# The second residual's addition on GpSimd instead of VectorE, with the layer norm statistics behind it as a step of their own

## The chip, the cores and the metric

One core of one Trainium2 chip runs the whole program. The metric is the device time of one execution in microseconds (us), and less is better. The engines are TensorE (PE in the profile, its weight loads PEld), VectorE (DVE), ScalarE (ACT), GpSimd (POOL) and SyncE (SP), which issues nearly all DMAs. Each works through its own queue of instructions in order and waits on semaphores for the others.

## The reference

Two layers work on x of shape 2 x 2048 x 512 in float32. The first has attention to a context of 128 rows and a feed-forward part with ternary weights. The second has a linear mixing part and a quantised feed-forward part. The piece that matters here is the second residual of the first layer and what reads it:

```
h  = bitlinear(ln2, w_fc) + gate * low_rank(ln2)
x2 = r1 + tanh(g_ffn[0]) * bitlinear(relu(h) ** 2, w_proj)   # second residual
y  = (x2 - mean(x2)) / sqrt(var(x2) + 1e-5)                  # the second layer's norm
x3 = x2 + tanh(g_xattn[1]) * (y @ W1.T + part2 + b)          # third residual
```

Here r1 is the result of the first residual (x plus the gated attention), and the layer norms have no weights.

## The kernel before, in words

The 4096 rows of x are cut into 16 groups of 256 rows, g = 0 to 15, and each group into two tiles t = 0, 1 of 128 rows. A tile of activations is 128 partitions x 512 float32. The weights are prepared in about the first 130 us, partly beside the first groups. From then on some four groups are under way at once: while one group is in its attention, the one before is in the first feed-forward part and older ones are in the second layer.

No scheduler runs on the chip. The table `ORDER` holds for each engine, each kind of step, each group and each tile the place of that step in the engine's queue. `moments` and `due` turn the table into the queues at build time, and each engine's `run` calls the steps in the order of those places. At one place a step may issue several instructions.

The steps around the change, for tile t of group g:

- `down` on PE multiplies the squared hidden values with w_proj into PSUM bank `FFN0 + t` and signals `down_ps`.
- `x2_out` on VectorE (lines 1454 to 1463) multiplies that bank with the row scales `scbc` into `r2` (line 1459) and signals `down_mul`; `low_rows` and `up` of the next group on PE wait for this signal, since they write the same banks. Then it adds `r1` to `r2` in place (line 1461), signals `x2_done`, and goes on in the same step to `ln_stats` (lines 1369 to 1374: statistics, a one-column memset, aggregate, and variance plus epsilon into `ve`).
- `rs3` on GpSimd (line 749) raises `ve` to the power -0.5 into `rs`.
- `ln3_apply` on VectorE (line 1378) forms the normalised `x3n`, ScalarE makes the float16 high part, `x3_lo` on GpSimd (line 753) the low part, SP turns both with a DMA transpose, and `mix` on PE multiplies them.
- `add_cb` on GpSimd (line 788) adds the context row `cb` to `r2` after `ln3_apply`.

GpSimd also runs `x1_lo` and `x2_lo` (line 753, low parts of the first and second normalised input), `hid` (line 776), `norm` (line 781), `rot` (line 771), `add_b2` (line 794) and the other `rs` steps. For the last group `r2_of` gives `xb` and the transposes are made by PE.

Of the kernel before, what the change touches and what calls it, by code (L numbers as in the profile page):

```python
# [48 lines left out]
def build(nc, x_d, ctxT_d, wqT_d, wkvT_d, woT_d, wfc_d, wproj_d, uT_d, wxT_d, wcT_d, bx_d, w1T_d, b1_d, w2T_d, b2_d,  # L49
          rope_d, small_d, out_d):  # L50
    ctx = ExitStack()
    with ctx:
# [278 lines left out]
        def last_in(place):  # L331
# [49 lines left out]
                rot_lo=((24, 27), (69, 70), (114, 115), (164, 165), (214, 215), (261, 265), (310, 312), (359, 361),  # L381
                        (410, 411), (456, 457), (505, 507), (554, 555), (602, 603), (653, 654), (704, 705),
                        (750, 751)),
                rot=((21, 25), (64, 66), (111, 112), (162, 163), (212, 213), (259, 262), (306, 309), (356, 358),
                     (407, 408), (452, 453), (502, 504), (552, 553), (600, 601), (650, 651), (702, 703),
                     (744, 745)),
                sum=((36, 39, 44, 45), (77, 80, 82, 84), (120, 132, 134, 135), (171, 173, 174, 183),
# [3 lines left out]
                max=((31, 32, 33, 38), (73, 74, 75, 76), (117, 121, 122, 124), (166, 167, 168, 169),  # L391
# [3 lines left out]
                p_lo=((40, 41, 47, 50), (87, 92, 93, 96), (123, 137, 138, 140), (175, 176, 180, 187),  # L395
# [3 lines left out]
                pv=((51, 57), (99, 105), (142, 144), (191, 192), (237, 242), (291, 292), (330, 339), (380, 389),  # L399
                    (434, 435), (486, 488), (536, 537), (584, 586), (627, 633), (682, 683), (730, 731), (779, 780)),  # L400
                x1=((59, 61), (107, 109), (149, 151), (197, 198), (246, 249), (295, 296), (342, 344), (393, 396),
                    (441, 442), (491, 493), (540, 542), (589, 591), (638, 640), (687, 688), (739, 740), (783, 785)),
                ln2=((60, 63), (110, 113), (150, 153), (199, 200), (248, 250), (298, 299), (346, 347), (395, 397),
                     (444, 445), (495, 496), (544, 547), (593, 594), (642, 643), (690, 691), (741, 742),
                     (787, 788)),
                low=((83,), (118,), (160,), (206,), (258,), (307,), (354,), (403,), (455,), (506,), (556,), (604,),
                     (652,), (697,), (749,), (796,)),
                q4=((119, 128), (170, 181), (211, 226), (260, 276), (314, 329), (362, 379), (409, 432), (466, 469),
                    (512, 523), (564, 570), (612, 619), (657, 665), (700, 711), (756, 770), (795, 798), (819, 822)),
                x3=((116, 125), (161, 177), (209, 220), (257, 271), (311, 324), (353, 375), (406, 425), (459, 468),  # L410
                    (508, 519), (558, 567), (608, 615), (649, 663), (699, 709), (753, 762), (793, 797), (818, 820)),
                h=((129, 130, 131, 133, 136, 146, 147, 148), (178, 184, 185, 186, 188, 189, 195, 201),
# [7 lines left out]
                q5_sc=((139, 157), (190, 207), (241, 251), (289, 303), (338, 357), (390, 401), (433, 449),  # L420
                       (485, 498), (535, 546), (583, 597), (632, 645), (679, 693), (728, 746), (775, 786),
                       (805, 809), (828, 833)),
                q5=((141, 159), (193, 210), (244, 255), (293, 305), (340, 360), (392, 404), (436, 451), (487, 500),
                    (538, 550), (585, 598), (634, 647), (681, 694), (738, 748), (781, 789), (806, 811), (832, 834)),
                x4=((154, 172), (205, 216), (253, 264), (304, 318), (350, 369), (402, 418), (454, 462), (499, 514),
                    (549, 563), (596, 609), (646, 656), (692, 706), (747, 757), (791, 794), (816, 821), (835, 836)),
                ln3=((104, 108), (145, 158), (196, 203), (240, 263), (301, 308), (343, 355), (387, 405), (440, 458),
                     (492, 503), (541, 551), (590, 605), (637, 655), (686, 701), (729, 752), (784, 792),
                     (812, 815)),
                x2=((102, 106), (143, 156), (194, 202), (238, 256), (294, 302), (341, 352), (385, 399), (437, 450),  # L430
                    (490, 501), (539, 548), (588, 599), (635, 648), (684, 695), (727, 743), (782, 790), (810, 813)),
                ln1_st=((0, 1), (14, 16), (62, 67), (126, 152), (179, 204), (221, 252), (272, 297), (327, 345),
                        (376, 398), (427, 443), (471, 494), (522, 543), (573, 592), (617, 641), (685, 696),
                        (732, 733)),
                ln1=((2, 4), (17, 18), (65, 68), (127, 155), (182, 208), (225, 254), (280, 300), (332, 348),
                     (382, 400), (431, 446), (475, 497), (526, 545), (579, 595), (625, 644), (689, 698),
                     (734, 735))),
# [41 lines left out]
                x1_lo=((2, 3), (9, 10), (30, 31), (73, 83), (107, 121), (139, 152), (173, 183), (209, 219),  # L479
                       (243, 254), (278, 286), (312, 319), (344, 353), (378, 388), (412, 422), (453, 459),  # L480
                       (486, 487)),
                x2_lo=((28, 29), (51, 55), (78, 82), (114, 115), (147, 149), (181, 182), (217, 218), (249, 251),
                       (285, 287), (321, 322), (355, 356), (387, 389), (421, 424), (454, 455), (490, 491),
                       (521, 522)),
                x3_lo=((49, 50), (76, 87), (111, 119), (144, 158), (185, 191), (214, 225), (246, 258), (281, 293),
                       (315, 327), (349, 361), (384, 395), (417, 431), (450, 465), (483, 498), (520, 525), (0, 0)),
                rot=((11, 12), (25, 26), (52, 54), (90, 92), (127, 129), (156, 157), (188, 190), (224, 227),
                     (259, 262), (290, 291), (324, 326), (359, 360), (392, 393), (428, 429), (467, 468),
                     (493, 494)),
                norm=((14, 15, 16, 17), (32, 33, 34, 35), (58, 70, 71, 72), (97, 98, 99, 105), (135, 136, 137, 140),  # L490
# [83 lines left out]
        def due(eng, name, p):  # L574

            return placed.get((eng, name, p), ())
# [1428 lines left out]
```

## Time and profile before

| what | value |
| --- | --- |
| median of 3 runs | 1177.62 us (1175.28 to 1179.0) |
| the profiled execution's own time | 1178.83 us |
| span of its instructions | 1176.7 us |
| PE busy | 1094.3 us, 93% |
| VectorE busy | 953.5 us, 81% |
| ScalarE busy | 799.4 us, 68% |
| GpSimd busy | 591.5 us, 50% |

The span runs from the first to the last instruction of the profiled execution. Its own time is 2.1 us longer, for what lies around the instructions, and is 1.2 us above the median of the runs. Busy time counts an engine's instructions without its waits, so a share well under 100% says nothing by itself about which wait sets the end.

### The profile page before, as it was taken

To read this page: it belongs to the slowest core of one execution; us is meant where nothing else is said; L and a number is where in the kernel's file an instruction comes from. 1 tells how busy PE (TensorE), PEld (TensorE's weight loads), DVE (VectorE), ACT (ScalarE), POOL (GpSimd) and SP (SyncE) were. 2 spreads that over 40 slices of the span, in tenths; PEclk is the share of its full clock that TensorE was granted. 3 is DMA by queue.
4 is the path that set the end of the run, shared out by engine and by line. 5 is a ranking of instruction groups with operands and counts; after the bars stand their busy time and mean duration, and the time that the engine had idled before them with its cause. 6 is when DMAs were issued, how large, how long until landed. Compare 5 with 4: busy or idle time off the path is not lost.

```text
span 1176.7 us, 22172 instructions
## 1 busy us (share of the span) xinstructions
PE 1094.3 (93%) x8270; PEld 677.4 (58%) x8558; DVE 953.5 (81%) x1989; ACT 799.4 (68%) x1575; POOL 591.5 (50%) x567
## 2 busy tenths in 40 slices
PE   5776699999999999999899999999999999999997
PEld 5544456474655656475655656475656656564654
DVE  4796868778789888788878798898879886998667
ACT  3988947676683958576584857676674957586545
POOL 4243545464653746454544656555545555564431
PEclk9888799999999999999999999999999999999999
DMA  9959651434525343533625252443436242432210
GB/s 339 367 153 309 204 122 47 99 81 77 126 59 117 69 116 73 104 81 68 126 53 136 57 123 68 89 110 77 108 55 145 45 119 61 103 69 55 68 45 27
DMA packets 273802, 128.11 MB, mean 109 GB/s; under 512 B 247568, under 2 KB 248080, under 8 KB 272016
## 3 DMA queue, kind: packets, MB, share of 16 engines
q1 hardware_dynamic: 273136, 125.73, 41.8%
q8 instruction: 67, 1.10, 0.4%
q10 hardware_dynamic: 560, 0.96, 0.3%
q14 instruction: 39, 0.32, 0.1%
HBM read 57.19 MB, written 8.39 MB: 56 GB/s over the span
## 4 chain that ended last, share of the span: by engine, by line
PE 55%; ACT 17%; DVE 16%; POOL 5%; issue 4%; DMA 2%; SPq 0%; ACTq 0%; DVEq 0%
PE ps L1861 14%; PE ps L1835 10%; PE ps L1904 6%; PE ps L1920 5%; PE ps L1788 5%; ACT e L966 4%; PE ps L1735 4%; PE ps L1883 4%; ACT rl L1002 3%; ACT hid L1007 2%; ACT sq L1013 2%; PE ps L1760 1%; DVE st L1369 1%; PE ps L1841 1%; PE ps L1775 1%
## 5 line engine op out<-in xcount | busy, mean ns | idle before, releaser
L1835 PE MATMUL ps<-xT,fcT 128*128 128x256 f16 x2048 | 262.5, 276 | 10.8 <-ACT rl L1002 7.1
L749 POOL TENSOR_TENSOR rs<-ve,nhalf 128x1 f32<-128x1 f32 x160 | 101.7, 638 | 306.1 <-DVE ve L1374 222.8
L1861 PE MATMUL ps<-pjT,hid 128*128 128x512 fp8e4 x1024 | 232.3, 379 | 2.6 <-POOL hid L776 1.6
L1835 PEld LDWEIGHTS ps<-xT,fcT 128*128 128x128 fp8e4 x2048 | 200.1, 99 | 52.6 <-ACT rl L1002 10.0
L776 POOL TENSOR_TENSOR hid<-sq,hid 128x512 f16<-128x512 f32 x128 | 163.1, 1279 | 80.3 <-ACT sq L1013 79.4
L1861 PEld LDWEIGHTS ps<-pjT,hid 128*128 128x128 f16 x1024 | 98.0, 98 | 98.3
L1002 ACT ACTIVATE rl<-ps,rsf 128x256 f32<-128x256 f32 x256 | 106.4, 469 | 25.0 <-PE ps L1841 24.8
L966 ACT ACTIVATE e<-ps,nmb,sig 128x128 f32<-128x128 f32 x256 | 113.1, 462 | 7.2 <-DVE nmb L1412 6.9
L1904 PE MATMUL ps<-w1T,q4T 128*128 128x512 fp8e4 x480 | 114.2, 379 | 0.7 <-issue 0.6
L1058 ACT ACTIVATE q<-h 128x2048 f16<-128x2048 f32 x30 | 57.3, 1910 | 79.3 <-DVE h L1531 79.3
L781 POOL TENSOR_TENSOR e<-e,einv 128x512 f32<-128x512 f32 x64 | 70.1, 1100 | 78.5 <-DVE einv L1416 78.5
L1520 DVE SCALAR_TENSOR_TENSOR h<-ps,dqs,b1bc 128x512 f32<-128x512 f32 x120 | 87.4, 744 | 27.0 <-PE ps L1904 24.4
L1920 PE MATMUL ps<-w2T,hT 128*128 128x512 fp8e4 x480 | 108.5, 379 | 0.7 <-DMA hT<-q 0.7
L1735 PE MATMUL ps<-pt,wq 128*128 128x256 f16 x768 | 88.6, 275 | 4.4 <-DVE r L1434 3.0
L1788 PE MATMUL ps<-wo,qT 128*128 128x512 f16 x384 | 87.3, 384 | 4.4 <-DVE qT L1382 4.4
L1735 PEld LDWEIGHTS ps<-pt,wq 128*128 128x128 f16 x768 | 75.3, 99 | 18.4 <-issue 7.8
L1883 PE MATMUL ps<-wx,xT 128*128 128x512 f16 x360 | 82.5, 379 | 2.3 <-DVE r L1556 1.2
L1007 ACT ACTIVATE hid<-rl 128x512 f16<-128x512 f32 x128 | 80.6, 630 | 5.0
L1100 DVE TENSOR_REDUCE amax<-h 128x1 f32<-128x2048 f32 x30 | 68.4, 2280 | 13.4 <-ACT h L1027 13.3
L1013 ACT ACTIVATE sq<-rl 128x512 f32<-128x512 f32 x128 | 78.5, 613 | 0.0
L1920 PEld LDWEIGHTS ps<-w2T,hT 128*128 128x128 f16 x480 | 46.2, 98 | 50.7
L1382 DVE TENSOR_TENSOR p<-e,p 128x512 f16<-128x512 f32 x64 | 62.6, 993 | 14.0 <-ACT p L974 13.7
(243 smaller groups left out, 2025.7 us busy)
## 6 DMA issues: line engine op xcount, KB each, us to landing
xb<-in_x SPq DMA_DIRECT2D x16, 512.0 KB, 3.6
xa<-in_x SPq DMA_DIRECT2D x15, 512.0 KB, 4.0
out<-r SPq DMA_DIRECT2D x30, 256.0 KB, 2.3
rope<-in_rope SPq DMA_DIRECT2D x16, 384.0 KB, 3.2
h<-in_w1T SPq DMA_DIRECT2D x6, 1024.0 KB, 5.8
h<-in_w2T SPq DMA_DIRECT2D x6, 1024.0 KB, 6.4
h<-in_wkvT SPq DMA_DIRECT2D x2, 1024.0 KB, 12.6
hid<-in_w_fc SPq DMA_DIRECT2D x2, 1024.0 KB, 9.9
```

The costliest lines, as they stand in the source:

```text
L776: pool.tensor_tensor(flat[:, 1, :], sq[:, m % 2, :], flat[:, 0, :], ALU.subtract).then_inc(hid_lo, 1)
L966: last = act.activation(e[:, n, a * S:(a + 1) * S], s_bank(g, n)[:, a * S:(a + 1) * S], ACT.Exp, bias=nmb[:, n, a:a + 1], scale=sig[:, :], ...
L1002: act.activation(rl[:, m % 2, a * G:(a + 1) * G], ps[:, FFN0 + m % 2, a * G:(a + 1) * G], ACT.Relu, scale=rsf[:, 2 * m + a:2 * m + a + 1]) ...
L1007: act.activation(hid[:, 0, 2 * m:2 * m + 2, :].rearrange("p c n -> p (c n)"), rl[:, m % 2, :], ACT.Square)\
L1013: act.activation(sq[:, m % 2, :], rl[:, m % 2, :], ACT.Square).then_inc(sq_done, 1)
L1735: mm = pe.matmul(q_bank(hg)[:, a * G:(a + 1) * G], wq[:, ws, k, c:c + P], xT1[:, xs, k, :], start=(n == 0 and k == 0), stop=(n == 2 and k ...
L1788: mm = pe.matmul(wo_bank(t), ao[:, xs, k, t * P:(t + 1) * P], wo[:, ws, k, :], start=(n == 0 and k == 0), stop=(n == 2 and k == KC - 1))
L1835: pe.matmul(ps[:, FFN0 + m % 2, a * G:(a + 1) * G], fcT[:, k, f * P:(f + 1) * P], xT2[:, xs, k, :], start=(xs == 0 and k == 0), stop=False)
L1861: mm = pe.matmul(ps[:, FFN0 + t, :], hid[:, xs, c, t * P:(t + 1) * P], pjT[:, c, :], start=(c == 0 and xs == 0), stop=(c == FC - 1 and xs ...
L1883: mm = pe.matmul(mix_bank(g, t), xT3_of(g)[:, xs, k, t * P:(t + 1) * P], wx[:, ws, k, :], start=(n == 0 and k == 0), stop=(n == 2 and k == ...
L1904: mm = pe.matmul(mix_bank(g, 2 + u), q4T_of(g)[:, k, t * P:(t + 1) * P], w1T[:, k, n * 512:(n + 1) * 512], start=(k == 0), stop=(k == KC - 1))
L1920: mm = pe.matmul(mix_bank(g, 10 + t), hT_of(g)[:, t, c, :], w2T[:, c, :], start=(c == 0), stop=(c == FC - 1))
```

## The change

On VectorE the addition of `r1` is taken out of `x2_out`, and the statistics become a step `x2_st` of their own. On GpSimd a new step `add_r1` makes the addition. The semaphores are the same: `add_r1` waits for `down_mul` and signals `x2_done`, and `x2_st` waits for `x2_done`. There are 32 of each, two for every group. Apart from the two new rows of the table, every engine runs its steps in the sequence that it had before; only the numbers of the places are shifted. PE, ScalarE and SP keep their places unchanged.

```diff
             DVE=dict(
+                x2_st=((103, 108), (146, 160), (199, 208), (245, 264), (303, 312), (352, 364), (398, 413),
...
             POOL=dict(
+                add_r1=((44, 47), (77, 86), (113, 121), (148, 160), (185, 193), (221, 231), (256, 266), (293, 304),
...
+            def add_r1(g, t):
+                need(pool, down_mul, TILES, g, t)
+                pool.tensor_tensor(r2_of(g)[:, t, :], r2_of(g)[:, t, :], r1[:, g % 2, t, :], ALU.add).then_inc(x2_done, 1)
+
...
                     for t, g in due("POOL", "x3_lo", p):
                         x3_lo(g, t)
+                    for t, g in due("POOL", "add_r1", p):
+                        add_r1(g, t)
...
                 need(dve, down_ps, TILES, g, t)
                 dve.tensor_tensor(r2_of(g)[:, t, :], ps[:, FFN0 + t, :], scbc[:, :], ALU.mult).then_inc(down_mul, 1)
-                need(dve, down_mul, TILES, g, t)
-                dve.tensor_tensor(r2_of(g)[:, t, :], r2_of(g)[:, t, :], r1[:, g % 2, t, :], ALU.add).then_inc(x2_done, 1)
+
+            def x2_stats(g, t):
                 need(dve, x2_done, TILES, g, t)
                 ln_stats(ln3, g, 2, t, r2_of(g)[:, t, :], 1.0, EPS)
...
                         x2_out(g, t)
+                    for t, g in due("DVE", "x2_st", p):
+                        x2_stats(g, t)
```

Where the new steps stand is shown at two places. The first is VectorE's queue around `x2_out` of group 8, tile 0 (about 685 us in the profile). Before, the multiplication, the addition (r<-r) and the statistics follow each other:

```order
L1531 TENSOR_SCALAR h<-h,qsc 128x2048
L1382 TENSOR_TENSOR qT<-ps,qT 128x2x256
L1520 SCALAR_TENSOR_TENSOR h<-ps,dqs,b1bc 128x512
L1459 TENSOR_TENSOR r<-ps,scbc 128x512
L1461 TENSOR_TENSOR r<-r 128x512
L1369 BN_STATS st<-r 128x6
L1371 MEMSET pad 128x1
L1372 BN_AGGR mv<-st 128x2
L1374 TENSOR_SCALAR ve<-mv 128x1
L1434 SCALAR_TENSOR_TENSOR r<-ps,kapo,xb 128x512
```

In the changed kernel the same stretch reads so, with lines shifted by 12:

```order
L1543 TENSOR_SCALAR h<-h,qsc 128x2048
L1394 TENSOR_TENSOR qT<-ps,qT 128x2x256
L1532 SCALAR_TENSOR_TENSOR h<-ps,dqs,b1bc 128x512
L1471 TENSOR_TENSOR r<-ps,scbc 128x512
L1381 BN_STATS st<-r 128x6
L1383 MEMSET pad 128x1
L1384 BN_AGGR mv<-st 128x2
L1386 TENSOR_SCALAR ve<-mv 128x1
L1446 SCALAR_TENSOR_TENSOR r<-ps,kapo,xb 128x512
```

The addition has gone, and nothing was put between the multiplication and the statistics. This holds at all 32 places: `x2_st` is the very next step behind its `x2_out`.

The second place is GpSimd's queue around the same step of group 13, tile 1 (about 1022 us), with `x1_lo` (x16a) and `x2_lo` (x16f) of group 14. Before:

```order
L753 TENSOR_TENSOR x16a<-xa,x16a 128x512 x2
L749 TENSOR_TENSOR rs<-ve,nhalf 128x1 x2
L753 TENSOR_TENSOR x16f<-rl,x16f 128x512 x2
L749 TENSOR_TENSOR rs<-ve,nhalf 128x1
L771 TENSOR_TENSOR e<-e 128x512 x2
```

In the changed kernel, where lines are shifted by 6 and L792 is the new addition:

```order
L759 TENSOR_TENSOR x16a<-xa,x16a 128x512 x2
L755 TENSOR_TENSOR rs<-ve,nhalf 128x1 x2
L759 TENSOR_TENSOR x16f<-rl,x16f 128x512
L792 TENSOR_TENSOR r<-r 128x512
L759 TENSOR_TENSOR x16f<-rl,x16f 128x512
L755 TENSOR_TENSOR rs<-ve,nhalf 128x1
L777 TENSOR_TENSOR e<-e 128x512 x2
```

Here the addition stands between the two `x2_lo` of group 14. At 27 of the 32 places it stands directly ahead of the `rs3` of its own tile. At the other five (tile 1 of groups 1, 4, 9, 13 and 14) another step of GpSimd lies between, in groups 9, 13 and 14 the `x2_lo` of the next group's tile 1.

## Rows read from the trace of the kernel before

**Rows 1.** The page: busy time of each engine, share of the span, instructions.

```profile
PE 1094.3 (93%) x8270; PEld 677.4 (58%) x8558; DVE 953.5 (81%) x1989; ACT 799.4 (68%) x1575; POOL 591.5 (50%) x567
```

**Rows 2.** Windows of the span: start and end, us, busy us of each engine, clock, DMA.

```profile
400.00:500.00 100.00, 98.09 (x702) 57.99 (x732) 83.23 (x166) 68.69 (x129) 54.53 (x52) 1.00 0.44 96
...
1000.00:1100.00 100.00, 97.59 (x685) 55.34 (x712) 88.43 (x185) 63.05 (x109) 51.15 (x50) 1.00 0.38 86
```

**Rows 3.** The chain that ended last, shares by engine and by line, from the page.

```profile
PE 55%; ACT 17%; DVE 16%; POOL 5%; issue 4%; DMA 2%; SPq 0%; ACTq 0%; DVEq 0%
```

**Rows 4.** That chain in order of time (start us, us): VectorE's additions on it.

```profile
298.90 0.70 DVE r L1461
...
433.05 1.26 DVE r L1461
...
1004.90 0.70 DVE r L1461
```

**Rows 5.** Lines, by form: count, busy us and mean ns of one, idle time before.

```profile
L749 POOL TENSOR_TENSOR rs<-ve,nhalf 128x1 f32<-128x1 f32 x160 | 101.7, 638 | 306.1 <-DVE ve L1374 222.8 <-DVE ve L1527 68.8 <-DVE ve L1543 14.3
...
L753 POOL TENSOR_TENSOR x16f<-rl,x16f 128x512 f16<-128x512 f32 x32 | 41.6, 1310 | 12.5 <-ACT x16f L984 12.5
...
L794 POOL TENSOR_TENSOR r<-r,b2bc 128x512 f32<-128x512 f32 x30 | 37.9, 1264 | 0.4 <-DVE x3n L1481 0.4
...
L1461 DVE TENSOR_TENSOR r<-r 128x512 f32<-128x512 f32 x30 | 23.0, 767 | 1.0
```

**Rows 6.** Timeline of VectorE, 684 to 690 us (start us, us; idle in brackets).

```profile
685.08 0.67 DVE L1459 TENSOR_TENSOR r<-ps,scbc 128x512 f32<-128x512 f32 x1
685.79 0.69 DVE L1461 TENSOR_TENSOR r<-r 128x512 f32<-128x512 f32 x1
686.51 0.69 DVE L1369 BATCH_NORM_STATS2 st<-r 128x6 f32<-128x512 f32 x1
...
687.46 0.15 DVE L1374 TENSOR_SCALAR ve<-mv 128x1 f32<-128x1 f32 x1
```

**Rows 7.** Timeline of GpSimd in the same stretch.

```profile
682.77 2.14 POOL L753 TENSOR_TENSOR x16a<-xa,x16a 128x512 f16<-128x512 f32 x1
687.70 0.55 POOL L749 TENSOR_TENSOR rs<-ve,nhalf 128x1 f32<-128x1 f32 x1 [2.79 <-DVE ve L1374]
```

**Rows 8.** Timeline of GpSimd, 1018 to 1032 us.

```profile
1021.10 0.80 POOL L749 TENSOR_TENSOR rs<-ve,nhalf 128x1 f32<-128x1 f32 x1 [1.25 <-DVE ve L1374]
1022.30 2.77 POOL L753 TENSOR_TENSOR x16f<-rl,x16f 128x512 f16<-128x512 f32 x2 [0.40 <-ACT x16f L984]
```

**Rows 9.** Timeline of VectorE in that stretch.

```profile
1021.93 0.55 DVE L1378 TENSOR_SCALAR rl<-r,mv,rs 128x512 f32<-128x512 f32 x1 [0.44 <-POOL rs L749]
...
1023.12 0.93 DVE L1461 TENSOR_TENSOR r<-r 128x512 f32<-128x512 f32 x1
```

**Rows 10.** SP's issues and PE there, and time to landing from the DMA view.

```profile
1023.57 2.80 SPq L650 DMA_TRANSPOSE xT<-x16f  x2
...
1028.81 0.40 PE L1801 MATMUL ps<-xT,vcol 128*32 128x256 f16 x8
...
xT<-x16f SPq DMA_TRANSPOSE x32, 2.8
```

**Rows 11.** VectorE, then GpSimd, 430 to 436 us: beside the long addition of the chain.

```profile
434.34 0.69 DVE L1369 BATCH_NORM_STATS2 st<-r 128x6 f32<-128x512 f32 x1
...
432.60 1.15 POOL L753 TENSOR_TENSOR x16a<-xa,x16a 128x512 f16<-128x512 f32 x1
```

**Rows 12.** Waits of PE, 300 to 1100 us: total us, times, longest.

```profile
PE ps L1760 <- DVE qT L1382: 5.7, 6, 2.0
```

**Rows 13.** Chain near the end, then VectorE's row that PE needs there.

```profile
1135.28 3.45 PE ps L1920 x16
...
1138.79 0.63 PE ps L1647 x4
...
1138.10 0.55 DVE L1378 TENSOR_SCALAR e<-xb,mv,rs 128x512 f32<-128x512 f32 x1
```

More of the change, by code:

```diff
@@ L401, in build @@
[L401 to L407, printed above, removed]
@@ L420, in build @@
[L420 to L424, printed above, removed]
@@ new lines, in build @@
+                rot_lo=((24, 27), (69, 70), (116, 117), (168, 169), (220, 221), (269, 273), (320, 322), (371, 373),
+                        (424, 425), (472, 473), (523, 525), (574, 575), (624, 625), (677, 678), (730, 731),
+                        (778, 779)),
+                rot=((21, 25), (64, 66), (113, 114), (166, 167), (218, 219), (267, 270), (316, 319), (368, 370),
+                     (421, 422), (468, 469), (520, 522), (572, 573), (622, 623), (674, 675), (728, 729),
+                     (772, 773)),
@@ new lines, in build @@
+                sum=((36, 39, 44, 45), (77, 80, 82, 84), (122, 134, 136, 137), (175, 177, 178, 187),
[3 rows of a table added]
+                max=((31, 32, 33, 38), (73, 74, 75, 76), (119, 123, 124, 126), (170, 171, 172, 173),
[3 rows of a table added]
+                p_lo=((40, 41, 47, 50), (87, 92, 93, 96), (125, 139, 140, 142), (179, 180, 184, 191),
[3 rows of a table added]
+                pv=((51, 57), (99, 106), (144, 147), (195, 196), (243, 249), (299, 300), (340, 349), (392, 402),
+                    (448, 449), (502, 504), (554, 555), (604, 606), (649, 655), (706, 707), (757, 758), (807, 808)),
@@ new lines, in build @@
+                x1=((59, 61), (109, 111), (152, 154), (202, 203), (253, 256), (304, 305), (353, 355), (406, 409),
+                    (456, 457), (508, 510), (559, 561), (610, 612), (661, 663), (712, 713), (766, 767), (812, 814)),
+                ln2=((60, 63), (112, 115), (153, 156), (204, 205), (255, 257), (307, 308), (357, 358), (408, 410),
+                     (459, 460), (512, 513), (563, 566), (614, 615), (665, 666), (715, 716), (768, 769),
+                     (816, 817)),
+                low=((83,), (120,), (164,), (212,), (266,), (317,), (366,), (417,), (471,), (524,), (576,), (626,),
+                     (676,), (723,), (777,), (826,)),
@@ new lines, in build @@
+                q5_sc=((141, 161), (194, 213), (248, 258), (297, 313), (348, 369), (403, 415), (447, 464),
+                       (501, 515), (553, 565), (603, 618), (654, 668), (703, 718), (755, 774), (803, 815),
+                       (835, 839), (860, 865)),
+                q5=((143, 163), (197, 216), (251, 262), (301, 315), (350, 372), (405, 418), (450, 467), (503, 517),
+                    (556, 570), (605, 619), (656, 670), (705, 719), (765, 776), (809, 818), (836, 842), (864, 866)),
@@ new lines, in build @@
+                ln1_st=((0, 1), (14, 16), (62, 67), (128, 155), (183, 210), (227, 259), (280, 306), (337, 356),
+                        (388, 411), (441, 458), (487, 511), (540, 562), (593, 613), (639, 664), (710, 722),
+                        (759, 760)),
+                ln1=((2, 4), (17, 18), (65, 68), (129, 158), (186, 214), (231, 261), (288, 309), (342, 359),
+                     (394, 414), (445, 461), (491, 514), (544, 564), (599, 616), (647, 667), (714, 724),
+                     (761, 762))),
@@ new lines, in build @@
+                x2_lo=((28, 29), (53, 57), (81, 85), (119, 120), (154, 156), (190, 191), (228, 229), (262, 264),
+                       (300, 302), (338, 339), (374, 376), (408, 410), (444, 447), (479, 480), (517, 519),
+                       (550, 552)),
+                x3_lo=((51, 52), (79, 91), (116, 125), (151, 166), (195, 201), (225, 237), (259, 272), (296, 309),
+                       (332, 345), (368, 381), (405, 417), (440, 455), (475, 491), (510, 526), (549, 555), (0, 0)),
+                rot=((11, 12), (25, 26), (54, 56), (94, 96), (133, 135), (164, 165), (198, 200), (236, 239),
+                     (273, 276), (306, 307), (342, 344), (379, 380), (414, 415), (452, 453), (493, 494),
+                     (521, 522)),
@@ new lines, in build @@
+                norm=((14, 15, 16, 17), (32, 33, 34, 35), (60, 72, 73, 74), (101, 102, 103, 109),
[3 rows of a table added]
+                rs2=((22, 23), (49, 55), (80, 82), (117, 118), (153, 155), (187, 188), (223, 226), (261, 263),
+                     (297, 298), (333, 334), (367, 371), (403, 406), (441, 442), (476, 477), (515, 516),
+                     (545, 547)),
+                rs3=((45, 48), (78, 88), (114, 122), (149, 161), (186, 196), (222, 232), (257, 267), (294, 305),
+                     (330, 341), (366, 377), (402, 413), (438, 449), (472, 483), (507, 520), (544, 553),
+                     (571, 574)),
@@ new lines, in build @@
+                add_b2=((59, 65), (97, 106), (129, 138), (163, 173), (205, 216), (234, 250), (275, 286), (311, 318),
+                        (347, 354), (383, 390), (420, 426), (451, 462), (487, 498), (529, 534), (557, 559),
+                        (577, 579)),
+                rs5=((76, 89), (112, 126), (152, 158), (184, 197), (220, 238), (260, 269), (291, 303), (326, 337),
+                     (364, 373), (399, 411), (436, 446), (469, 481), (508, 523), (542, 548), (565, 569),
+                     (580, 581)),
```

94 lines of the change are left out of this document (30 added, 64 removed), and 52 rows, old and new, of tables (h, hid, max, norm).

## Prediction, made before the changed kernel had run

> **What bounds the kernel now.** I read the page first: PE is busy 93% of the span, VectorE 81%, GpSimd 50% [rows 1]. Such shares are means over a start, a steady part and an end, so I split the span into windows. In the steady part PE is busy 98 of 100 us, VectorE 83 to 88 of 100 [rows 2]. PE is the bound there, and VectorE is the next in line, with little room. Then I read the chain that ended last. PE has only 55% of it, VectorE 16%, ScalarE 17%, GpSimd 5% [rows 3]. PE's long pieces are joined again and again by short stretches over the other engines, which can't be seen in PE's idle time, since PE fills part of them with other work. PE's own waits for VectorE show where these joints hurt: from 300 to 1100 us the largest entry is 5.7 us in six waits for `qT` [rows 12]. So VectorE isn't the bound by its busy time, but a delay of VectorE at the wrong moment is paid.
>
> Next I looked for the step that is changed on the chain. Ten of the 32 additions of line 1461 lie on it, the first at 298.90 and the last at 1004.90 us, one of them a long one of 1.26 us at 433.05 [rows 4]. At these ten places VectorE went through multiplication, addition and statistics without a pause, and the end of the program hung on it.
>
> **What the change removes and adds, on VectorE.** The usual case is in [rows 6]: the multiplication ends at 685.08 + 0.67 = 685.75, the addition takes 0.69, and the statistics start at 686.51, which is 0.76 us behind the multiplication's end. After the change VectorE has nothing between the two and waits for GpSimd. That takes:
> - the hand-over to GpSimd, 0.09 us: `ve` ended at 687.46 + 0.15 = 687.61 and GpSimd's `rs` that waited for it started at 687.70 [rows 6, 7];
> - the addition on GpSimd. This very one isn't in the trace. The nearest row is line 794, the same shape, types and operation with two inputs: 1.26 us [rows 5]. As bounds I take VectorE's own time, 0.69, below, and line 753 of `x16f` with its collisions, 1.31, above [rows 5, 6]. I take 1.26;
> - the hand-over back, 0.03 us: `rs` ended at 1021.10 + 0.80 = 1021.90, and VectorE's instruction behind it started at 1021.93 [rows 8, 9].
>
> The sum is 1.38 us in place of 0.76, so the statistics start **0.62 us later**, and everything that is queued behind them on VectorE with them: in this place the `x1_out` of the next group, for whose sum and norm PE's next low-rank and up products wait. Taking 0.69 us of work from VectorE thus makes VectorE's queue longer, since its place is not filled. The 32 places make 32 x 0.62 = 20 us of delay.
>
> **On GpSimd.** It gets 32 x 1.26 = 40 us more work, 591.5 to about 632 us, still 54% of the span. That alone costs nothing: the `rs` steps wait 306 us in total, 222.8 of it for `ve` [rows 5], and the addition falls into the wait that stood there. In [rows 7] GpSimd ended `x16a` at 682.77 + 2.14 = 684.91, before the multiplication's end, and then sat idle for 2.79 us. At six places it is still at work at that moment by more than a hair, mostly with `x16f`. The worst on the chain is the one at 433.05: `x16a` ends at 432.60 + 1.15 = 433.75, so the statistics would start at 433.75 + 1.26 + 0.03 = 435.04 instead of 434.34 [rows 11], 0.7 later, and 0.8 if the hand-over counts in full. All 32 together come to some 21 us.
>
> In three groups the new addition also stands ahead of the second `x2_lo` of the next group. In group 13 the pair ran from 1022.30 to 1025.07 [rows 8]. With an addition of 1.26 us between them, and the low parts at 1.15 like the undisturbed `x16a` of [rows 11], it ends near 1025.9, 0.8 later. SP turns the result (2.8 us to landing), which was there by about 1027.9, and PE reads it at 1028.81 [rows 10]. The room is 0.9, so nearly used up. I count 0.2 us for it, with 0 to 1 as bounds. No DMA is added or moved on SP; the transposes of x3 start later by the same 0.6 us as the norm.
>
> **A rule on the other side.** The added work on GpSimd also frees VectorE's second read path. The trace shows the collision: the addition takes 0.93 us at 1023.12, while GpSimd is in its `x16f` pair, and 1.26 at 433.05 [rows 4, 9], against 0.69 alone; the group's mean is 767 ns [rows 5]. So the additions lose (0.767 - 0.69) x 30 = 2.3 us this way, and GpSimd's `x16f`, at 1.31 [rows 5] against 1.15 [rows 11], may lose up to 0.16 x 32 = 5.1 us, not all of it by this.
>
> The Trainium skill (SBUF — State Buffer, section Who interferes with whom) says that a VectorE instruction with two SBUF inputs contends with a GpSimd instruction that reads SBUF, and that the one that starts second blocks for the whole of the other. The trace agrees with 0.93 and 1.26 us against 0.69. By this rule alone the change would win up to 2.3 + 5.1 = 7 us; by the sum of waits it loses, and the new GpSimd addition collides with nothing on VectorE, which is waiting for it.
>
> **The sum.** On the chain: nine places x 0.62 = 5.6, and 0.8 for the tenth, 6.4 us. These are paid in full unless the chain is only the last of several equals, and even then a chain made longer stays longer. The last group's second tile adds 0.5: PE's turn of its norm starts at 1138.79, VectorE's row ended at 1138.10 + 0.55 = 1138.65, and PE's work before ended at 1135.28 + 3.45 = 1138.73, so the room is 0.1 us [rows 13]. The shifted `x2_lo` adds 0.2. Of the other 20 places some will become the last to arrive; I take 0.9 us for them, as an estimate, like one and a half of 20 places. Together **8 us**. Against the profiled execution, 1178.83 us, that is 1186.8. The median of the runs is 1.2 us lower, so the forecast is **1185.7 us**.
>
> **Rivals.**
> - *The cover holds.* VectorE's idle time of 12 to 17 us in 100 [rows 2] takes up the 0.62 us before PE needs anything. For it: from one `x2_out` to the next there are some 30 us with about 4 us of idle time. Against it: ten of the places lie on the chain. It would give 0 to 3 us more, 1178 to 1181.
> - *All places are paid.* Each delay reaches PE, because queues written out by hand for one timing have no spare room anywhere. Then 21 us, and 1199 us in the median. For it: PE at 98%, so that nothing lost is given back. Against it: 22 of the 32 additions aren't on the chain. Half-way, at 13 us and more, I count it as this case.
> - *Faster, by fewer collisions.* The mechanism is the read path above: VectorE's additions no longer stop GpSimd's low parts and the reverse. It gives 2 to 7 us less, about 1173 to 1175. It decides if the hand-over and the longer addition cost less than 0.2 us on the chain in each place, thus if GpSimd did the addition in about 0.8 us. Line 794 with 1.26 speaks against it.
>
> **How the numbers follow.** A measurement of this kernel tells about 0.3%, 3.5 us, from no change. The forecast's case (4 to 13 us more) gets 0.62; all places paid 0.14; the cover holds 0.15; faster 0.09. The last two give same 0.15 and faster 0.09, the first two slower 0.76. The range goes from 1179 (the cover nearly holds) to 1195 (17 us more, four fifths of all places); it leaves out the faster case and the upper part of the second rival, some 2 in 10.
>
> **What the new profile would show.** If right: VectorE's statistics on `r` at the new step wait 32 times for GpSimd's new line, 1.3 to 1.4 us each, 42 to 46 us in total; VectorE's busy time falls by 22 to 25 us while its waits grow by about twice that; the new addition takes 1.26 to 1.30 us; GpSimd's wait of `rs` for `ve` falls by 20 to 40 us; PE's busy time is unchanged, and its waits for VectorE (`qT`, `r`, `x3n` for the turn at the end) grow by some 6 to 10 us in all. The chain has pieces of GpSimd's new line, about ten or more. The forecast is wrong low if PE's waits grow by over 13 us, or if GpSimd comes to the addition late at many places, by 1 us or more. It is wrong high if VectorE's wait is there in full and PE's waits don't grow. If the clock granted to PE, 1.00 in the steady windows [rows 2], falls in longer pauses of PE, the time would be longer for a reason that isn't in this sum.

## The result, and the profile after

| | median us | runs | ratio to the kernel before |
| --- | --- | --- | --- |
| before | 1177.41 (1175.28 to 1179.0) | 4 | |
| changed | 1188.84 (1187.55 to 1192.19) | 4 | 1.0111, 95% interval 1.0085 to 1.0138 |

The change makes the kernel 11.4 us slower (forecast 8 us, 1185.7 us, in a range of 1179 to 1195). The page of the changed kernel has these lines against [rows 1, 3]: the span, busy times, and the chain's shares.

```profile
span 1188.0 us, 22172 instructions
...
PE 1093.6 (92%) x8270; PEld 673.0 (57%) x8558; DVE 926.8 (78%) x1957; ACT 799.8 (67%) x1575; POOL 629.3 (53%) x599
...
PE 30%; ACT 27%; DVE 24%; POOL 11%; issue 5%; DMA 3%; SPq 0%; ACTq 0%; DVEq 0%
```

PE's work is the same, VectorE has 27 us less to do and GpSimd 38 us more, and the program is longer. PE's share of the chain fell from 55% to 30%, VectorE's rose from 16% to 24% and GpSimd's from 5% to 11%. In two windows of the steady part (columns as in [rows 2]) PE loses 0.9 and 1.5 us in 100, VectorE has more idle time than before, and the clock granted to PE is 1.00 as it was:

```profile
400.00:500.00 100.00, 97.22 (x697) 57.61 (x728) 79.89 (x171) 70.29 (x139) 59.20 (x58) 1.00 0.39 88
1000.00:1110.00 110.00, 105.68 (x720) 58.88 (x753) 90.84 (x194) 71.43 (x139) 59.19 (x58) 1.00 0.36 82
```

Where VectorE's idle time went is in the lines of the changed kernel (columns as in [rows 5]):

```profile
L755 POOL TENSOR_TENSOR rs<-ve,nhalf 128x1 f32<-128x1 f32 x160 | 101.6, 638 | 220.9 <-DVE ve L1386 137.3 <-DVE ve L1539 68.7 <-DVE ve L1555 14.3
...
L1381 DVE BATCH_NORM_STATS2 st<-r 128x6 f32<-128x512 f32 x92 | 63.9, 694 | 47.2 <-POOL r L792 45.0
...
L759 POOL TENSOR_TENSOR x16f<-rl,x16f 128x512 f16<-128x512 f32 x32 | 40.0, 1258 | 15.4 <-ACT x16f L996 15.1
...
L792 POOL TENSOR_TENSOR r<-r 128x512 f32<-128x512 f32 x30 | 38.0, 1267 | 59.8 <-DVE r L1471 59.7
```

The new addition takes 1267 ns; the working had 1264 from line 794. The statistics on `r` waited 47.2 us, 45.0 of that for the addition. With the last group's two tiles it is 47.8 us in 32 waits, by the view of line 792. That view gives the waits of GpSimd before the addition (total us, times), then who waited for it:

```profile
  DVE r L1471: 59.7, 22
  DVE xb L1471: 0.5, 1
...
  DVE st L1381: 47.8, 32
```

The first two lines are under "its engine sat idle before it", the third under "who waited for it". GpSimd was idle before 23 of 32 additions, ready when VectorE's multiplication ended. `rs` waits 137.3 us for `ve` instead of 222.8. Of the difference of 85.5 the addition took over 60.2 as its own wait, and filled the rest. `x16f` became shorter, 1258 ns instead of 1310.

The place of [rows 6, 7] in the changed kernel, VectorE first, then GpSimd (timeline, idle time in brackets):

```profile
689.79 0.68 DVE L1471 TENSOR_TENSOR r<-ps,scbc 128x512 f32<-128x512 f32 x1
691.84 0.69 DVE L1381 BATCH_NORM_STATS2 st<-r 128x6 f32<-128x512 f32 x1 [1.38 <-POOL r L792]
...
692.79 0.15 DVE L1386 TENSOR_SCALAR ve<-mv 128x1 f32<-128x1 f32 x1
```

```profile
687.49 2.14 POOL L759 TENSOR_TENSOR x16a<-xa,x16a 128x512 f16<-128x512 f32 x1
690.54 1.26 POOL L792 TENSOR_TENSOR r<-r 128x512 f32<-128x512 f32 x1 [0.92 <-DVE r L1471]
693.02 0.55 POOL L755 TENSOR_TENSOR rs<-ve,nhalf 128x1 f32<-128x1 f32 x1 [1.22 <-DVE ve L1386]
```

The multiplication ends at 690.47, GpSimd adds from 690.54 to 691.80, and the statistics start at 691.84. That is 1.37 us behind the multiplication, against 0.76 before: 0.61 later, where the working had 0.62. Added up over all 32 places the statistics start 47.8 us behind the multiplications, against 26.6 before: 21.2 us of delay, of which the program pays about half.

For [rows 8, 10], the pair of `x2_lo` in group 13 with the addition between them, on GpSimd and then what PE did:

```profile
1031.38 1.20 POOL L759 TENSOR_TENSOR x16f<-rl,x16f 128x512 f16<-128x512 f32 x1 [0.40 <-ACT x16f L996]
1032.55 1.27 POOL L792 TENSOR_TENSOR r<-r 128x512 f32<-128x512 f32 x1
1033.78 1.15 POOL L759 TENSOR_TENSOR x16f<-rl,x16f 128x512 f16<-128x512 f32 x1
```

```profile
1034.35 3.62 PE L1934 MATMUL ps<-w2T,hT 128*128 128x512 fp8e4 x16
1037.90 0.40 PE L1815 MATMUL ps<-xT,vcol 128*32 128x256 f16 x8
```

The second `x2_lo` ends at 1034.93. It is 9.9 us later than before while PE's reading (line 1815) is 9.1 us later; it follows the work in front of it at 1037.97 without a pause. The room was enough.

Near the end the chain now runs through the new line (chain in order of time, answering to [rows 13]):

```profile
1145.40 0.70 DVE xb L1471
...
1146.17 1.27 POOL xb L792
...
1147.46 0.69 DVE st L1381
```

The new addition lies on the chain at 26 of its 32 places. PE's own waits for VectorE, 300 to 1100 us, are larger than in [rows 12] (total us, times, longest):

```profile
PE ps L1774 <- DVE qT L1394: 8.3, 7, 1.9
PE ps L1897 <- DVE r L1568: 3.4, 4, 1.7
```

All of PE's waits for VectorE in that stretch went from 9.9 us to 17.1, 7.2 more, within the 6 to 10 of the prediction.

### The profile page after: what moved, and what is told of

Its sections match the earlier page's. It is cut to its first block, busy times and chain, and to the rows that moved or that the text cites. A ratio compares the mean times of both kernels' runs of the same rounds, so it can differ in the third digit from the quotient of the medians.

```text
span 1188.0 us, 22172 instructions
## 1 busy us (share of the span) xinstructions
PE 1093.6 (92%) x8270; PEld 673.0 (57%) x8558; DVE 926.8 (78%) x1957; ACT 799.8 (67%) x1575; POOL 629.3 (53%) x599
## 4 chain that ended last, share of the span: by engine, by line
PE 30%; ACT 27%; DVE 24%; POOL 11%; issue 5%; DMA 3%; SPq 0%; ACTq 0%; DVEq 0%
PE ps L1849 7%; PE ps L1875 6%; ACT e L978 6%; ACT rl L1014 4%; DVE st L1381 3%; DVE amax L1112 3%; PE ps L1918 3%; ACT hid L1019 3%; ACT sq L1025 3%; PE ps L1934 3%; POOL r L792 3%; PE ps L1897 2%; ACT h L1039 2%; DVE h L1543 2%; POOL rs L755 2%
## 5 line engine op out<-in xcount | busy, mean ns | idle before, releaser
L1849 PEld LDWEIGHTS ps<-xT,fcT 128*128 128x128 fp8e4 x2048 | 198.6, 99 | 55.6 <-ACT rl L1014 11.2
L755 POOL TENSOR_TENSOR rs<-ve,nhalf 128x1 f32<-128x1 f32 x160 | 101.6, 638 | 220.9 <-DVE ve L1386 137.3
L1381 DVE BATCH_NORM_STATS2 st<-r 128x6 f32<-128x512 f32 x92 | 63.9, 694 | 47.2 <-POOL r L792 45.0
L1749 PEld LDWEIGHTS ps<-pt,wq 128*128 128x128 f16 x768 | 74.2, 98 | 20.7 <-issue 11.4
```

The source lines that it names most:

```text
L755: pool.tensor_tensor(rs[:, n, t:t + 1], ve[:, n, t:t + 1], nhalf[:, :], ALU.pow).then_inc(done, 1)
L1749: mm = pe.matmul(q_bank(hg)[:, a * G:(a + 1) * G], wq[:, ws, k, c:c + P], xT1[:, xs, k, :], start=(n == 0 and k == 0), stop=(n == 2 and k ...
L1849: pe.matmul(ps[:, FFN0 + m % 2, a * G:(a + 1) * G], fcT[:, k, f * P:(f + 1) * P], xT2[:, xs, k, :], start=(xs == 0 and k == 0), stop=False)
```

## The experiments

Twelve runs. The medians compare each kernel with the kernel before on the same chip. Beside them I read each profile in one more way. The multiplication of `x2_out` is done 32 times in every kernel, and the time from its first start to its last leaves out the preparation of the weights and the end. I call this time the distance. Here are the two rows that give it for the kernel before, profiled a second time in e5 (start of the first and last in us), and for the changed kernel:

```profile
L1459 DVE TENSOR_TENSOR r<-ps,scbc x30: 674/684/693, 157.2 to 1081.1; 128x512 f32<-128x512 f32 x30
L1459 DVE TENSOR_TENSOR xb<-ps,scbc x2: 682/687/692, 1124.6 to 1131.4; 128x512 f32<-128x512 f32 x2
```

```profile
L1471 DVE TENSOR_TENSOR r<-ps,scbc x30: 673/684/693, 158.2 to 1095.0; 128x512 f32<-128x512 f32 x30
L1471 DVE TENSOR_TENSOR xb<-ps,scbc x2: 681/686/692, 1138.6 to 1145.4; 128x512 f32<-128x512 f32 x2
```

It is 1131.4 - 157.2 = 974.1 us before and 1145.4 - 158.2 = 987.2 after, 13.1 more. The first profile of the kernel before has 1134.9 - 158.3 = 976.6; 1.7 of its 2.4 us more came between tile 1 of group 6 and tile 0 of group 7 (55.4 us against 53.7), so this stretch varies from run to run. All distances below are against 974.1.

A distance belongs to one execution, and not always to a middling one. The profiled execution of e1 took 1180.34 us where the median is 1184.89, and that of e11 1202.90 where the median is 1207.59. The starts of the multiplications also show what each place costs, as the growth of the time from its multiplication to the next. For tile 0 of group 8, from the timeline of VectorE, before and after:

```profile
682.32 0.67 DVE L1459 TENSOR_TENSOR r<-ps,scbc 128x512 f32<-128x512 f32 x1
...
697.00 0.68 DVE L1459 TENSOR_TENSOR r<-ps,scbc 128x512 f32<-128x512 f32 x1
```

```profile
689.79 0.68 DVE L1471 TENSOR_TENSOR r<-ps,scbc 128x512 f32<-128x512 f32 x1
...
705.07 0.68 DVE L1471 TENSOR_TENSOR r<-ps,scbc 128x512 f32<-128x512 f32 x1
```

The step is 14.68 us before and 15.28 after: this place is paid with 0.60 us. Read so for all 31 steps, the changed kernel pays 6.3 us at the ten places of the old chain, 6.7 us at twelve others, and 0.1 us at the last nine.

The 6.7 us have to be split. At nine of the twelve the two profiles of the kernel before agree within 0.14 us, and the changed kernel pays 4.8 us there. At the other three (tile 0 of group 0, tile 1 of groups 6 and 11) the two profiles of the kernel before differ by 0.6, 1.7 and 0.7 us, and the changed kernel's 1.9 us can't be told from that. With them left out the sum is 6.3 + 4.8 + 0.1 = 11.2 us, close to the 11.4 of the medians.

| run | ratio, 95% interval | in us | first to last multiplication |
| --- | --- | --- | --- |
| e1, the ten of the chain | 1.0085 (1.0069 to 1.0101) | +10.0 | +6.0 |
| e12, the same again | 1.0061 (1.0049 to 1.0073) | +7.2 | +7.6 |
| e2, the other 22 | 1.0080 (1.0065 to 1.0094) | +9.4 | +8.3 |
| e3, 0.6 us of VectorE more | 1.0107 (1.0089 to 1.0126) | +12.6 | +11.3 |
| e4, statistics a step later | 1.0138 (1.0123 to 1.0153) | +16.2 | +15.5 |
| e5, before again | 0.9996 (0.9984 to 1.0007) | -0.5 | 0 (the reference) |
| e6, no addition | 0.9966 (0.9956 to 0.9976) | -4.0 | -2.8 |
| e7, addition twice | 1.0010 (1.0000 to 1.0020) | +1.2 | +2.4 |
| e8, nine places, later | 0.9992 (0.9982 to 1.0002) | -0.9 | +0.1 |
| e9, the ten free places | 1.0013 (0.9999 to 1.0026) | +1.5 | +1.3 |
| e10, 0.2 us of VectorE more | 1.0044 (1.0030 to 1.0058) | +5.2 | +5.1 |
| e11, 1.2 us of VectorE more | 1.0262 (1.0240 to 1.0284) | +30.8 | +27.4 |

"In us" is the ratio's excess times the median of the kernel before beside it (1175.07 for e1 to e4, 1176.67 for e5 to e8, 1176.53 for the rest). These three sets were timed on three different chips.

**Which places pay: e1, e2, e9, e12.** GpSimd adds at a part of the places, VectorE at the others:

```diff
+        ON_CHAIN = ((2, 1), (3, 0), (3, 1), (4, 1), (6, 0), (7, 1), (8, 0), (12, 0), (12, 1), (13, 0))
+
+        def by_pool(g, t):
+            return (g, t) in ON_CHAIN
...
             def add_r1(g, t):
+                if not by_pool(g, t):
+                    return
...
                 dve.tensor_tensor(r2_of(g)[:, t, :], ps[:, FFN0 + t, :], scbc[:, :], ALU.mult).then_inc(down_mul, 1)
+                if not by_pool(g, t):
+                    need(dve, down_mul, TILES, g, t)
+                    dve.tensor_tensor(r2_of(g)[:, t, :], r2_of(g)[:, t, :], r1[:, g % 2, t, :], ALU.add).then_inc(x2_done, 1)
```

e2 has `not in`; e9 has the ten places at which the changed kernel lost nothing, as its expectation lists them.

> GpSimd makes the addition only at the ten places whose addition lay on the chain of the kernel before; at the other 22 VectorE makes it as before. Theory A (each place that is paid costs the 0.62 us of VectorE's wait, and the chain tells which ones are): 6.5 us over the kernel before, as in the changed kernel between these places. Theory B (the loss is a matter of how much the addition costs in all, no matter where): 10 of 32 parts of 11.4, so 3.6 us. Theory C (GpSimd's shifted queue, above all the additions ahead of the next group's low parts, which are not among these ten): 2 us or less.

> The complement: GpSimd makes the addition only at the 22 places off the chain. Theory A as I predicted it (the others are hidden but for near ties): 1.6 us over the kernel before. Theory A as the changed kernel's times between the places read, with near ties much more frequent: about 5 us. Theory B: 22 of 32 parts of 11.4, so 7.8 us. Theory C: nearly all of 11.4, 9 us or more.

Measured: +10.0 and +9.4 us by the medians. Theory B fails on the ten places: it gives 3.6 us, and a third of the places costs about as much as the other two thirds. The 22 by themselves would fit it (7.8 in an interval of 7.6 to 11.0). Theory C fails: the ten places, which hold none of the shifted `x2_lo`, cost clearly more than 2 us. Theory A fails with few near ties (1.6 us for the 22) and holds with many: its about 5 us fits the steps of e2 below, though not e2's median. The first rows of e1 are

```profile
L1478 DVE TENSOR_TENSOR r<-ps,scbc x30: 674/684/693, 156.6 to 1086.5; 128x512 f32<-128x512 f32 x30
L1478 DVE TENSOR_TENSOR xb<-ps,scbc x2: 680/686/692, 1130.0 to 1136.8; 128x512 f32<-128x512 f32 x2
```

1136.8 - 156.6 = 980.2, so +6.0 between the multiplications, 5.4 of it at the ten places themselves. e2 has +8.3, 7.9 of it at the twelve: 4.8 at the nine of them that are steady, as in the changed kernel, and 3.1 at the three that vary. At the nine, e1 has 0.0. Together the distances make 14.4, near the 13.1 of the changed kernel. The medians add up to more (19.4). A part of that is which execution was profiled: e1's was the shortest of four, and is 5.3 us over the kernel before.

> The kernel in which GpSimd adds only at the ten places of the old chain, once more. Its profile had 6.0 us over the kernel before between the first and the last multiplication, but its median was 9.8 us over. If the median holds 3 to 4 us that come from the start of the program in that session, it is now 5 to 7 us over; if they belong to the kernel, 9 to 10 us again.

Measured: +7.2 by the median and +7.6 by the distance, 5.9 at the ten places and 1.6 in the stretch of group 6 that varies. The intervals of the two medians, 8.1 to 11.9 us in e1 and 5.8 to 8.6 here, just touch, so whether a part of the 10.0 belonged to e1's session isn't shown. The steps at the ten places agree better: 5.4 and 5.9 us here, 6.3 in the changed kernel. I take 5.5 to 6.5 us for them. That the medians of the two parts (7.2 or 10.0, and 9.4) add up to more than the 11.4 of the whole stays open; the whole has an interval of 10.0 to 16.2.

> GpSimd adds only at the ten places at which the changed kernel lost nothing by its trace (the time from this multiplication of x2_out to the next is within 0.12 us of the kernel before): tile 1 of groups 0, 1, 9, 14 and 15, tile 0 of groups 2, 4, 5, 7 and 15. If the loss is made place by place and adds up, this costs nothing: 0 to 1 us, within the noise. If the loss is one of VectorE's load as a whole, it costs ten 32nds of it, 3.5 us.

Measured: +1.5 us, with an interval from -0.1 to 3.1, and +1.3 by the distance. The 3.5 us of a loss by load lie just outside the interval. With the steps of e1 and e2 this says that the loss is made place by place.

**Is it VectorE's wait: e3, e10, e11.** The addition stays on VectorE, and an instruction whose result nobody reads delays the statistics:

```diff
                 need(dve, x2_done, TILES, g, t)
+                dve.bn_stats(spare[:, :], r2_of(g)[:, t, :])
                 ln_stats(ln3, g, 2, t, r2_of(g)[:, t, :], 1.0, EPS)
```

e10 reads only columns 0 to 127, and e11 has two such lines with two outputs.

> The kernel before, with the addition on VectorE as it was and a second bn_stats of the same tile (0.69 us, its result unused) ahead of the first at all 32 places. GpSimd's queue is the old one. If the whole loss is VectorE's later statistics and what is queued behind them, this costs 0.70 / 0.62 of the changed kernel's 11.4 us, so 12 to 14 us. If GpSimd's added 1.26 us and its shifted steps carry a part, it costs clearly less than the changed kernel, 8 us or less.

> The kernel before with a bn_stats of 128 columns instead of 512 ahead of the statistics, about 0.2 us at each of 32 places. If 16 places have no room at all and the others 0.1 us or more, this costs 16 x 0.2 = 3 us and a little for the others, 3 to 4 us. If VectorE had a room of some tenths of a us at most places, it costs 0 to 1 us.

> The kernel before with two more bn_stats of 512 columns, about 1.3 us at each of 32 places. If the 16 places without room and the six with 0.1 to 0.4 us of room are all (22 places pay the second 0.69 us in full), it costs the 11.3 us of one bn_stats and some 15 more, 26 us. If the other ten places have no room either beyond 0.6 us, it costs 11.3 + 22 = 33 us. If the idle time of VectorE takes up more, under 22 us.

The delays came out smaller than their instructions, since a second bn_stats starts before the first has ended. VectorE's rows in e3, then in e10 (timeline):

```profile
686.94 0.69 DVE L1464 BATCH_NORM_STATS2 spare<-r 128x6 f32<-128x512 f32 x1
687.55 0.68 DVE L1370 BATCH_NORM_STATS2 st<-r 128x6 f32<-128x512 f32 x1
```

```profile
686.57 0.29 DVE L1464 BATCH_NORM_STATS2 spare<-r 128x6 f32<-128x128 f32 x1
686.78 0.68 DVE L1370 BATCH_NORM_STATS2 st<-r 128x6 f32<-128x512 f32 x1
```

The true statistics start 0.61 us behind the spare ones in e3 and 0.21 in e10. So e3 delays by just what GpSimd's addition does at a usual place, with GpSimd's queue as it was. Over all 32 places it is 19.0 us, against 21.2 with GpSimd, which comes late at some. e3 costs 12.6 us (interval 10.5 to 14.8; 11.3 by the distance: 5.5 at the ten places and 5.7 at the twelve) against 11.4 (13.1). At the nine steady places it pays 4.6 us where the changed kernel pays 4.8. The delay of VectorE's queue accounts for the loss. It moves the statistics and all steps behind them alike, so e3 doesn't say which of them PE waits for. The difference between the two distances, 13.1 and 11.3, lies mostly in two steps: 0.7 at tile 1 of group 4, where GpSimd was late, and 0.4 at tile 1 of group 6, in the stretch that varies.

e10 pays 0.18 to 0.20 us of its 0.21 at eleven of the 31 steps and more at four, two of which are steps that vary. It costs 5.2 us by the median (interval 3.5 to 6.8) where the expectation was 3 to 4; of the 5.1 us by the distance 1.8 is the varying stretch. e11 pays 1.16 to 1.19 at twelve places, and six of the nine places that were free begin to pay, 3.0 us together. In all it is 30.8 us (27.4), between the 26 and the 33 of the two readings.

**What VectorE's time is worth the other way: e6.** No engine adds `r1`:

```diff
                 need(dve, down_mul, TILES, g, t)
-                dve.tensor_tensor(r2_of(g)[:, t, :], r2_of(g)[:, t, :], r1[:, g % 2, t, :], ALU.add).then_inc(x2_done, 1)
-                need(dve, x2_done, TILES, g, t)
                 ln_stats(ln3, g, 2, t, r2_of(g)[:, t, :], 1.0, EPS)
```

> The kernel before with the addition of r1 left out on every engine (the second residual isn't added); everything else in place. VectorE is 0.76 us earlier at each of 32 places. If VectorE's queue is on the path at most of these places, this wins what the delay lost, per us: 0.76 / 0.62 of 11.4 us, up to 14 us. If the path's joints are near ties with other engines, a gain ends at the next tie: 3 to 7 us. If VectorE's queue isn't the cause: 0 to 1 us.

```profile
span 1171.3 us, 22140 instructions
...
PE 1090.6 (93%) x8270; PEld 676.0 (58%) x8558; DVE 927.5 (79%) x1957; ACT 799.8 (68%) x1575; POOL 589.2 (50%) x567
```

Measured: -4.0 us (span and busy times above, -2.8 by the distance), the middle of the three. The statistics start 0.03 us behind the multiplication instead of 0.76, so they are 0.73 us earlier at a usual place, and 25.5 us in all. That wins a third of what e3's 19.0 us later costs. With the queues in this order, no way of taking the addition from VectorE should win more.

**GpSimd's load by itself: e7.** VectorE adds as before, and GpSimd makes the same addition into a dead buffer:

```diff
             def add_r1(g, t):
-                need(pool, down_mul, TILES, g, t)
-                pool.tensor_tensor(r2_of(g)[:, t, :], r2_of(g)[:, t, :], r1[:, g % 2, t, :], ALU.add).then_inc(x2_done, 1)
+                need(pool, x2_done, TILES, g, t)
...
+                pool.tensor_tensor(bxbc[:, :], r2_of(g)[:, t, :], r1[:, g % 2, t, :], ALU.add).then_inc(c_const, 1)
```

> The kernel before, with VectorE's addition kept, and GpSimd making the same addition once more into a buffer that is dead by then, at the places of the changed kernel, behind x2_done. VectorE waits for none of these. GpSimd has 40 us more work, and its steps behind it (the low parts of the next group in groups 9, 13 and 14, rs3) start up to 1.3 us later. If GpSimd's load and order carry a part of the loss, it shows here: 3 us or more. If VectorE's wait is all: 0 to 3 us, since rs3 starts about 0.2 us later than before.

```profile
L755 POOL TENSOR_TENSOR rs<-ve,nhalf 128x1 f32<-128x1 f32 x160 | 102.7, 645 | 185.8 <-DVE ve L1390 104.6 <-DVE ve L1545 66.5 <-DVE ve L1561 14.3
...
L796 POOL TENSOR_TENSOR bxbc<-r 128x512 f32<-128x512 f32 x30 | 38.5, 1284 | 80.8 <-DVE r L1477 80.8
```

Measured: +1.2 us (0 to 2.4). The 38.5 us of line 796 are there, in waits that `rs` had before (185.8 instead of 306.1 in all), and nearly nothing is paid. GpSimd's work and the shifted steps explain at most 2.4 of the 11.4 us.

**Work for VectorE while GpSimd adds: e4, e8.** The queue of VectorE is written anew after the table:

```diff
+                n = steps.index(("x2_st", g, t))
+                if steps[n + 1] != ("ln3", g, t):
+                    steps[n], steps[n + 1] = steps[n + 1], steps[n]
```

> The changed kernel with each statistics step of VectorE one step later in its queue, behind the step that followed it (31 of 32 places; at one the next step is the norm that needs the statistics). That step, 0.7 to 3 us long, runs while GpSimd adds, so VectorE's wait of 1.4 us goes at most places, and VectorE has 0.69 us less to do at each. If VectorE's queue is the cause, the wait for GpSimd falls from 48 us to 15 or less and the time to the kernel before or below it: 1171 to 1178 us. If the later norm (its start moves by the length of the step put ahead) is just as near the path, it stays at 1183 to 1190 us.

Measured: +16.2 us (interval 14.4 to 18.0). I had expected the opposite. VectorE's waits (total, times, longest) show that the wait for the addition has nearly gone, 5.3 us of 45:

```profile
DVE r L1462 <- PE ps L1818: 13.9, 9, 2.4
...
DVE x3n L1406 <- POOL rs L771: 11.9, 18, 0.7
...
DVE st L1397 <- POOL r L808: 5.3, 9, 1.4
```

But VectorE's idle time as a whole didn't fall: 257.5 us, against 258.7 in the changed kernel (the idle times in front of all its instructions, added up). The wait came back elsewhere. The step put ahead was often not ready itself. Where it is `x1_out` (line 1462) it waits for PE, 13.9 us instead of the 4.5 of the changed kernel, and all the steps put ahead together wait 25 us, with the statistics queued behind them. At tile 0 of group 8, for example, the timeline of VectorE shows 1.76 us of it, and the statistics start 2.54 us behind the multiplication instead of 1.38:

```profile
687.37 0.67 DVE L1487 TENSOR_TENSOR r<-ps,scbc 128x512 f32<-128x512 f32 x1
689.80 0.75 DVE L1462 SCALAR_TENSOR_TENSOR r<-ps,kapo,xb 128x512 f32<-128x512 f32 x1 [1.76 <-PE ps L1818]
690.58 0.69 DVE L1397 BATCH_NORM_STATS2 st<-r 128x6 f32<-128x512 f32 x1
```

Behind the statistics the norm `x3n` waits 11.9 us for `rs`, since it stands one or two steps behind. So the place in VectorE's queue was filled with a wait for PE in place of the wait for GpSimd, and the statistics, with the third residual's branch, started later still. The distance shows it at the twelve places (+11.3) more than at the ten (+2.4). Which consumer of that branch is the one that's late I haven't shown.

e8 does this only at nine places where the norm stands three or more steps behind (tile 1 of groups 3, 4, 6, 7, 10, 11, 12, 13 and tile 0 of group 4); VectorE adds at the other 23.

> GpSimd adds only at nine places at which VectorE's norm ln3_apply stands three or more steps behind the multiplication, and there VectorE's statistics come one step later, so that it has work while GpSimd adds; at the other 23 places VectorE adds as before. If the later statistics lost time in the run before (16 us) because the norm stood close behind at most places, this wins VectorE's 0.69 us at nine places, some of it on the path: 0 to 4 us less than the kernel before. If any later statistics are paid, or if the work put ahead is itself on the path, it is 2 to 6 us slower.

Measured: -0.9 us, interval -2.1 to +0.2, and +0.1 by the distance, which holds 2.3 us of the stretch of group 6 that varies (and is one of the nine places itself). The later statistics cost nothing there that can be told, and VectorE's 0.69 us at nine places gains nothing that can be told from no change. No version that still makes the addition beats the kernel before clearly.

**The control: e5.**

> The kernel before, unchanged, under a new name. It says how far two timings of one kernel lie apart, since the ten places and the 22 places alone came to 9.8 and 10.1 us, more than any theory of one sum allows (all 32 together 11.4). If the medians are sound, it comes out at 1.000 with an interval that holds 1, and its profile has 976 to 977 us between the first and the last x2_out multiplication, as the first profile (158.32 to 1134.88 us). If the start (weights, loads, clock) differs by some us from run to run, only the time before the first multiplication moves.

Measured: 0.9996, and 974.1 us between the multiplications where the first profile has 976.6. The interval is -1.9 to +0.8 us with ten runs, so a median of few runs isn't known to better than 1 to 2 us. A single profile's distance isn't better than 2 us, mostly for the one stretch.

## Why the prediction was right, and where it was off

**The price of a place** was right: 0.62 us worked out, 0.61 at the place of [rows 6], and the addition's 1.26 us measured 1.27. Reading the hand-overs (0.09 and 0.03 us) and a like instruction was enough. The sum over all places was right too: some 21 us, 21.2 measured.

**The ten places on the chain** were right: 6.4 us worked out, 6.3 measured in the changed kernel. At the tenth (tile 1 of group 4) GpSimd came later than I had worked out. The statistics start 2.62 us behind the multiplication instead of 1.32, so 1.30 later and not 0.7 to 0.8, but only 0.9 us was paid.

**The term that was sized wrong** is "Of the other 20 places some will become the last to arrive; I take 0.9 us for them". It measured 4.8 us at nine places, and up to 6.7 with the three steps that vary in the kernel before too. This is nearly all of the 3.4 us by which the forecast of 8 fell short. Four of the nine pay 0.6 us or more and had no room; five pay 0.4 to 0.5 and had 0.1 to 0.2 us of it. The old chain showed none of them. The chain is one path of many that end within a few tenths of a us of each other. Nothing that I had read spoke for one and a half of 20; e10 shows that even 0.21 us is paid in full or nearly so at about half of the places. The rival "all places are paid" named the reason, queues without spare room, but went too far: 19 places pay for certain, three can't be judged, and nine don't (the last place's step can't be read).

**The tail** was to add 0.5 us. From the last multiplication to the end of the span it is 1176.7 - 1134.9 = 41.8 us in the first profile before, 42.7 in the second and 42.6 after. The term can't be told from the variation.

**The shifted `x2_lo`** (0.2 us): the pair ended 9.9 us later and its reader started 9.1 later without a wait. The room of 0.9 us was read rightly. In e7 these shifts cost nothing that can be told.

**GpSimd's load** was right: 40 us forecast, 40.5 measured for the 32 additions (38 in all, since other steps became shorter), hidden. The new profile's sign for it was wrong: I said that the wait of `rs` for `ve` would fall by 20 to 40 us. It fell by 85, because the addition now does much of the waiting that `rs` did. VectorE's busy time fell by 27 us where I had 22 to 25, and its wait is 47.8 us where I had 42 to 46. I had counted six places at which GpSimd is still at work when the multiplication ends. The trace of the kernel before has seven: tile 1 of group 6, with an `rs` of 0.5 us, is missing.

**Fewer collisions** (the rival that ends faster): the collisions did get fewer, `x16f` went from 1310 to 1258 ns and VectorE's long additions are gone. The Trainium skill (SBUF — State Buffer, Who interferes with whom) says that a VectorE instruction with two SBUF inputs contends with a GpSimd instruction that reads SBUF. The traces agree: before, the six of the 32 additions that overlapped one of GpSimd's low parts took 0.93 to 1.44 us, and the others 0.69. Fewer collisions were worth 1.6 us of GpSimd's busy time on `x16f`, and the program got longer all the same. In e6, with the addition gone from both engines, this and the shorter queue together gave 4.0 us. The prediction's figure for this rival doesn't follow from its own terms: 2 to 7 us less is 1171 to 1176, not 1173 to 1175.

**The cover holds** was true of nine places and false of at least 19.

The sum itself, 1186.8 - 1.2, is 1185.6 and not 1185.7, which changes nothing.

## What to carry to other kernels

Moving an instruction to an engine that is idle doesn't unload the first one if the next instruction there waits for the result. The length of the wait (both hand-overs and the slower engine's time) replaces the work, unless another step fills it.

The chain that ended last gave a lower bound for the delay here (6.3 of 11.4 us). In a kernel whose queues were fitted to one timing, as many places again can be as tight. Price a delay at all places, look for those with proven room, and expect a small delay to be paid at many of them (here 0.21 us in full, or nearly, at 13 of the 28 steps that don't vary). The way back brings much less (here a third), most likely because the next path is close behind.

Before another step is put into a wait, check that its inputs are there by then. In e4 they often weren't.

## What the runs showed that I had not expected

- The response is one-sided: 0.73 us less at a usual place gives -4.0 us, 0.21 more +5.2, 0.61 more +12.6, 1.22 more +30.8.
- A second bn_stats of 128x512 behind a first delays what follows by 0.61 us and not by its 0.69, and one of 128x128, shown with 0.29 us, by 0.21: the next starts before it has ended.
- Giving VectorE the next step in place of the wait was no faster than the wait itself (+16.2 against +11.4 us, with intervals of 14.4 to 18.0 and 10.0 to 16.2), since that step often waited for PE.
